# A two-layer relational graph convolution on one core: relation 0 treated like the other seven, and the root product moved to the end of each layer

## The reference

```
x: 1250 x 768, edges: 21250 (src, dst, type 0..7), sorted by dst
layer(x, W[8], root, b):
    sums[dst, r]  = sum of x[src] over the edges of type r that end in dst
    mean          = sums / max(count, 1)
    return sum_r mean[:, r] @ W[r]  +  x @ root + b
h   = relu(layer(x, W1, root1, b1))
out = layer(h, W2, root2, b2)
result = layernorm(x + out)
```

## Time and profile before

| | |
|---|---|
| median of 3 runs | 1470.09 us |
| the profiled execution, its own time | 1469.78 us |
| its span, first to last instruction | 1468.0 us |
| PE busy | 1451.5 us, 99% of the span |
| DVE busy | 983.4 us, 67% |
| ACT busy | 604.9 us, 41% |
| POOL busy | 572.6 us, 39% |
| HBM read and written | 204.47 MB and 65.49 MB |

### The profile page before, as it was taken

The page is one execution under the profiler, slowest core; times in us unless marked ns, Lnnn a source line. Parts: engine busy times, 40 slices in busy tenths (PEclk is TensorE's granted clock), DMA queues, the critical chain, the costliest instruction groups (busy, mean ns, idle before and its releaser), DMA issues.

```text
span 1468.0 us, 23940 instructions
## 1 busy us (share of the span) xinstructions
PE 1451.5 (99%) x8875; PEld 1438.4 (98%) x8875; DVE 983.4 (67%) x1604; ACT 604.9 (41%) x845; POOL 572.6 (39%) x457
## 2 busy tenths in 40 slices
PE   8999999999999999999999999999999999999998
PEld 8999999999999999999999999999999999999997
DVE  8899999857777677898740144545454454539887
ACT  4222344335444443566342233334343333417654
POOL 0000000066777774764306233434242424316553
PEclk9999999999999999999999999999999999999999
DMA  6453321358777786565337465646464656625454
GB/s 200 146 169 124 94 76 43 105 183 267 255 208 247 238 250 188 150 192 165 105 122 216 151 207 170 207 146 218 141 212 151 212 169 189 214 82 149 145 168 132
DMA packets 109595, 249.70 MB, mean 170 GB/s; under 512 B 20183, under 2 KB 83334, under 8 KB 109442
## 3 DMA queue, kind: packets, MB, share of 16 engines
q0 software_dynamic: 32480, 135.65, 31.5%
q1 hardware_dynamic: 77026, 112.88, 23.7%
HBM read 204.47 MB, written 65.49 MB: 184 GB/s over the span
## 4 chain that ended last, share of the span: by engine, by line
PE 94%; DMA 2%; DVE 2%; ACT 1%; issue 1%; SPq 0%; POOL 0%; ACTq 0%; POOLq 0%; DVEq 0%
PE prod L872 72%; PE agg L918 15%; PE agg L1039 2%; PE agg L872 2%; PE prod L863 1%; DMA raw<-y,bucket_index 1%; PE prod L918 1%; DMA y<-y_stage 1%; DVE g_low L1166 1%; PE agg L863 0%; DMA x_rows<-in_x 0%; PE agg L1042 0%; DVE g_low L1170 0%; ACT g_high L705 0%; DVE g_high L1166 0%
## 5 line engine op out<-in xcount | busy, mean ns | idle before, releaser
L872 PE MATMUL prod<-w_high,h_high 128*128 128x384 f32 x2100 | 707.8, 337 | 0.0
L872 PE MATMUL prod<-w_high,h_low 128*128 128x384 f32 x2100 | 702.5, 335 | 0.0
L872 PE MATMUL prod<-w_low,h_high 128*128 128x384 f32 x2100 | 701.8, 334 | 0.0
L590 POOL DMA_INDIRECT raw<-y,bucket_index x346 | 448.7, 1297 | 506.6 <-DVE g_low L1170 249.8
L1170 DVE TENSOR_TENSOR g_low<-raw,g_high 128x768 fp32r<-128x768 f32 x246 | 225.5, 954 | 300.7 <-ACT g_high L708 299.6
L741 ACT ACTIVATE y_stage<-prod 128x384 f32<-128x384 f32 x280 | 137.7, 492 | 679.5 <-PE prod L872 670.3
L872 PEld LDWEIGHTS prod<-w_high,h_high 128*128 128x128 f32 x2100 | 394.3, 188 | 0.3 <-issue 0.2
L872 PEld LDWEIGHTS prod<-w_low,h_high 128*128 128x128 f32 x2100 | 394.5, 188 | 0.0
L872 PEld LDWEIGHTS prod<-w_high,h_low 128*128 128x128 f32 x2100 | 394.2, 188 | 0.0
L708 ACT ACTIVATE g_high<-raw 128x768 fp32r<-128x768 f32 x266 | 211.6, 839 | 64.4 <-PE agg L918 46.2
L918 PE MATMUL agg<-g_high,one_hot 128*128 128x384 f32 x720 | 186.0, 339 | 4.2 <-DVE g_low L1170 2.7
(11 more groups left out here) (178 smaller groups left out, 1002.6 us busy)
## 6 DMA issues: line engine op xcount, KB each, us to landing
y<-y_stage SPq DMA_DIRECT2D x280, 168.0 KB
w_raw<-in_w_all SPq DMA_DIRECT2D x35, 1152.0 KB, 7.2
raw<-y,bucket_index POOLq DMA_INDIRECT x346, 4.8
y<-y_stage SPq DMA_DIRECT2D x280, 19.5 KB
y<-in_x SPq DMA_DIRECT2D x1, 3750.0 KB, 14.0
acc<-in_x POOLq DMA_DIRECT2D x10, 375.0 KB, 4.3
x_rows<-in_x SPq DMA_DIRECT2D x10, 336.0 KB
y<-acc SPq DMA_DIRECT2D x10, 336.0 KB
```

The lines of the kernel that those rows point to most:

```text
L590: pool.indirect_dma_start(raw_rows(slot), None, y[0:written * N, :], bass.IndirectOffsetOnAxis(ap=bucket_index[:, at_column:at_column + 1] ...
L872: mm = pe.matmul(to, left[:, k, t * P:(t + 1) * P], right[:, h, k, :], start=(k == 0 and left is h_high and right is w_high), stop=(n == 0 ...
```

## The change

All eight relations are multiplied first, stored, gathered and summed in the same way. Relation 0 has two blocks a tile like the others, and its overflow joins the two shared overflow blocks at the last relation. `average`, `keep`, the turns of the averages, the copy of x and the store of h are gone. Layer 1 is now q = 0 to 7 for relations 0 to 7 and q = 8 for the root; layer 2 is q = 9 to 16 and q = 17 for the root. Both root matrices have the form that only q = 17 had: halves interleaved tile by tile, and relation 7's sums added onto the same banks. The order of the first steps is another: three steps of half 0, two of half 1, and then the buckets of tiles 0 and 1 directly after one another. In layer 1 the finished tile goes through relu and is turned there, and POOL may load x over a tile of `acc` as soon as that tile is turned. In `finish`, DVE cuts the low parts of the next tile before the moments of the last.

The diff, cut to its core:

```diff
-    TILES = [FULL] * (R - 2) + [FULL + 1, FULL + OVER]
+    TILES = [FULL] * (R - 1) + [FULL + OVER]
-    ROOT1 = R - 1
-    MEAN1 = R
-    ROOT2 = 2 * R
-    MEAN2 = Q - 1
+    ROOT1 = R
+    ROOT2 = Q - 1
-        PAIRED = BEHIND[R - 2]
+        PAIRED = LAYER
...
         def last_part(s):
+            if s < 5:
+                return ((0, 0), (0, 1), (0, 2), (1, 0), (1, 1))[s]
+            if s == STEPS - 1:
+                return 1, T - 1
+            return 1 - s % 2, (s + 1) // 2 - (1 - s % 2)
         def last_pair(t):
+            return (agg[:, 0, :, 0:HALF], prod[:, 0:2, 0:HALF], prod[:, 2:4, 0:HALF])[t % 3]
         def finished(s):
+            h, t = last_part(s)
+            return [0, 1] if s == 4 else [t] if s > 4 and h == 1 else []
+        def finishing(layer):
             def actions(s):
+                todo = [("sum", layer * R + R - 1, R - 1, t) for t in finished(s)]
+                if layer == 0 and s > 4:
+                    todo += [("turn", 1, None, t) for t in ([0] if s == 5 else [n - 1 for n in finished(s)])]
                 return todo
...
-                if s == STEPS - 1:
-                    sp.dma_start(y[0:N, :], x).then_inc(x_copied, 16)
...
-            for t in range(T):
-                sp.wait_ge(relu_done, t + 1)
-                for rows in parts_of(t):
-                    sp.dma_start(y[t * NT + rows.start:t * NT + rows.stop, :], acc[rows, t, :]).then_inc(h_stored, 16)
...
-            gather_relation(R - 1, R - 1, stop=SOONER)
-            pool.wait_ge(x_copied, 16)
-            gather_relation(R - 2, 0, 1)
-            gather_spilled(0, R - 1)
-            gather_relation(R - 1, R - 1, start=SOONER)
+            gather_spilled(0, R - 1)
             wait_y(0, R - 1)
+            gather_relation(R - 1, R - 1)
             def load_residual(t):
+                pool.wait_ge(transposed, 2 * T + 2 * (t + 1))
                 pool.dma_start(acc[0:ROWS[t], t, :], x[t * NT:t * NT + ROWS[t], :]).then_inc(residual_loaded[t], 16)
-            pool.wait_ge(transposed, 6 * T)
-            pool.wait_ge(h_stored, 16 * PARTS * T)
...
+            def finish(layer):                     # ScalarE
+                q, g = (ROOT1, ROOT2)[layer], layer * R + R - 1
+                high_of_unit(q, 1)
+                high_spilled(layer, g)
+                bucket(g, 0)
+                for t in range(T):
+                    if layer == 0 and t == T - 2:
+                        high_of_unit(q + 1, 0, STEPS * q + FIRST_HALF)
+                    if t + 1 < T:
+                        bucket(g, t + 1)
+                    if layer == 0:
+                        relu(t)
+                        if t:
+                            high_of_turn(1, t - 1)
+                    else:
+                        deviation(t)
+                        if t + 1 < T:
+                            norm(t)
...
+            def finish(layer):                     # TensorE
+                for s in range(STEPS):
+                    last_step(layer, s)
+                    for what, a, _, t in finishing(layer)(s):
+                        if what == "turn":
+                            turn(a, t)
+                        else:
+                            bucket(a, t, last_pair(t))
+                    if s == 0:
+                        sum_spilled(layer, layer * R + R - 1)
...
-            def keep(k, t, h, bank):
-                dve.wait_ge(prod_done, k + 1)
-                a = acc[:, t, h * HALF:(h + 1) * HALF]
-                dve.tensor_tensor(a, prod[:, bank, 0:HALF], a, ALU.add).then_inc(root_kept, 1)
...
+            def finish(layer):                     # VectorE
+                q, g = (ROOT1, ROOT2)[layer], layer * R + R - 1
+                low_of_unit(unit(q, 1), 1)
+                add_spilled(layer, g)
+                prepare(g, R - 1, 0)
+                for t in range(T):
+                    if layer == 0 and t == T - 2:
+                        low_of_unit(unit(q + 1, 0), 0)
+                    if t + 1 < T:
+                        mark(g, R - 1, t + 1)
+                        cut_low(g, t + 1, 0, 1)
+                    add(g, R - 1, t)
+                    if t + 1 < T:
+                        cut_low(g, t + 1, 1)
+                    if layer:
+                        moments_of(t)
+                        if t + 1 < T:
+                            scale_of(t)
+                    elif t:
+                        low_of_turn(1, t - 1)
```

More of the change, by code:

```diff
@@ L843, in norm @@
                                scale=std[:, t % 2, 1:2]).then_inc(normed, 1)
-            last = 2 * R - 1
-            high_of_unit(MEAN2, 1)
-            high_of_turn(3, T - 1)
-            high_spilled(1, last)
-            bucket(last, 0)
-            for t in range(T):
-                if t + 1 < T:
-                    bucket(last, t + 1)
-                deviation(t)
-                if t + 1 < T:
-                    norm(t)
+            matrix(2, 2, after=copied_ahead(2))
+            matrix(3, 3, after=copied_ahead(3))
+            for q in range(TABLE_END, ROOT1 - 1):
+                matrix(q, q, pair_of(q))
+            matrix(ROOT1 - 1, ROOT1 - 1, one_relation(R - 2, None))
+            finish(0)
+            matrix(ROOT1 + 1, stored_before(1, 0), last_turns)
+            with act.Fori(1, R) as r:
+                matrix(r + ROOT1 + 1, stored_before(1, r), one_relation(r + R - 1, None))
+            finish(1)
         @block.tensor
@@ new lines, in sum_spilled @@
+                        with pe.Fori(0, NB) as key:
+                            pe.wait_ge(spill_low[layer], i + 1)
+                            pe.wait_ge(spill_hot[layer], i * NB + key + 1)
+                            for part in (g_high, g_low):
+                                for c in range(2):
+                                    mm = pe.matmul(agg[:, 1, c, 0:HALF], one_hot[:, 0, 0, :],
+                                                   part[:, 0, c * HALF:(c + 1) * HALF],
+                                                   start=part is g_high, stop=part is g_low, skip_group_check=True)
+                            mm.then_inc(spill_summed[layer], 1)
@@ L1064, in matrix @@
                         middle[1]()
-                    if bank is None:
-                        last_step(s)
-                    else:
-                        step(q, s, bank(s), free(s))
+                    step(q, s, free(s))
                     if after:
@@ L1196, in low_of_turn, with matrix @@
                     low_of_half(u, t, turned(n, hh, t))
-            def matrix(q, actions, keep_step=None, more=True, spilled=None, after=None,
-                       low_at=((2, 0, K), (12, 0, K))):
-                cut = SPILL_STEP[spilled[0]] if spilled else -1
-                order = [(s, a[1:]) for s in range(STEPS) for a in actions(s) if a[0] != "turn"]
+            def matrix(q, actions, low_at=((2, 0, K), (12, 0, K))):
+                order = [a[1:] for s in range(STEPS) for a in actions(s) if a[0] == "sum"]
                 ready = n = 0
-                def prepare_next():
-                    prepare(*order[n][1])
-                    return n + 1
                 for s in range(STEPS):
-                    if keep_step and not spilled and s == max(0, order[0][0] - EARLY):
-                        ready = prepare_next()
-                    if keep_step:
-                        keep_step(s)
                     for what, *a in actions(s):
@@ L1218, in matrix @@
                             continue
-                        ahead = n + 1 < len(order) and not (s <= cut < order[n + 1][0])
-                        for m in range(ready, n + 1 + ahead):
-                            prepare(*order[m][1])
-                        ready = n + 1 + ahead
+                        for m in range(ready, min(n + 2, len(order))):
+                            prepare(*order[m])
+                        ready = min(n + 2, len(order))
                         n += 1
-                        if what == "sum":
-                            if keep_step:
-                                dve.wait_ge(root_kept, (STEPS if q == MEAN1 else 0) + s + 1)
-                            add(*a)
+                        add(*a)
                     for at, first, stop in low_at:
```

433 lines of the change are left out of this document (110 added, 323 removed).

## The result

The kernel after takes 1461.05 us (median of 4 runs, 1460.23 to 1461.29). The kernel before, beside it on the same chip, takes 1470.05 us (4 runs, 1469.45 to 1471.24). The ratio is 0.9938 with a 95% interval of 0.9922 to 0.9954. So it is faster by 9.0 us, where I had forecast 19.1, and it lies 3 us above the upper end of my range.

What follows compares the result with a forecast made beforehand. PE, busy 1451.5 of 1468.0 us, was taken to bound the kernel; 1469.8 less 24.9 saved, plus 4.1 for tiles 0 and 1 and 2.0 for early x, gave 1451.0 us, range 1446 to 1458.

Steps and rivals of the forecast that it cites:

- The table: Edge-column table matmuls: 20 of 480 columns go in each of 170 groups, saving 1.4 us.
- -13.6: Turns of averages: twenty turns, ten in each layer, leave PE at 0.68 us each, saving 13.6 us.
- -6.9: Third blocks of relation 0: 40 summing matmuls leave PE, saving 6.9 us.
- -3.0: Dense sums in q = 7: waits for rows and low parts, and before a first turn, vanish, saving 3.0 us.
- Are relation 7's rows there in time?: Closing stages, tile 0: a gather chain of 15.5 us fits within 17.0 us, so it costs 0.
- Rival 4: Kernel becomes slower: relation 7's rows arrive late in both layers, up to 1474 us; chance 0.04.
- Tiles 0 and 1 directly after one another: +4.1: Closing stages: tile 1's parts are made only during tile 0's bucket, costing 2.0 us a layer, 4.1 with latencies.
- x loaded early in layer 1: +2.0: End of q = 8: POOL's bias adds fall on tiles 8 and 9 and may hold DVE, costing 2.0 us, bounds 0 to 6.4.
- The other tiles: 0: Closing stages' remaining tiles: cadence 8.68 us in q = 17, 9.36 in layer 1, hides DVE and ACT work; costs 0.
- the last tile ... may bring 0 to 1 us and is left out: Kernel's end: low parts cut before the moments may bring 0 to 1 us, left out of the sum.
- the second: Rival: POOL's adds hold tiles 8 and 9 fully, +6.4, or one layer's gathers are late; 1455 to 1458 us; chance 0.20.
- the third: Rival: layer 1's closing stage settles at a DVE or ACT cadence of 10.2 us; 1459 to 1463 us; chance 0.08.

Runs made afterwards that it cites:

- e7_spaced: Kernel after with x loaded late, q = 17 moments before three low parts except tile 0's, and tiles 0, 1, 2 summed one step apart in both closing stages: 1451.73 us.
- e8_layer1: Kernel after with x loaded late, q = 17 moments before three low parts except tile 0's, and tiles 0, 1, 2 spaced in q = 8 alone: 1451.17 us.
- e1_late: Kernel after, but POOL loads x only when all of h is turned, so its adds leave the closing stage: 1449.48 us.
- e4_moments: Kernel after, but in layer 2 alone DVE takes a tile's moments ahead of the next tile's last three low parts; x loads stay early: 1458.08 us.
- e9_norm: Kernel after with x loaded late and ACT taking the previous tile's norm just ahead of this tile's deviation; moments stay last: 1450.80 us.

## Why the prediction was wrong

**Right: what bounds it, and the savings.** PE did lose the work, and the span followed PE and its waits and nothing else. The table gave 1.5 us (I had 1.4): ten of its edge columns take 2.02 us in place of 2.11 from start to start, and there are 17 such bursts. The sums have 1400 matmuls at L810, 40 fewer. q = 7 takes 76.3 us, exactly what q = 10 to 16 take, so the dense sums' waits are gone with their arrangement. The steps after the turns of averages, "-13.6", "-6.9" and "-3.0", gave together 14.1 + 9.4 + 0.8 = 24.3 us where I had 23.5. The rest is 3.9 in q = 0 to 6, in place of 1.4; 1.7 of that is q = 6, whose first step had taken 4.30 us before and takes 3.12 after.

**Right: "Are relation 7's rows there in time?"** Bucket 0 starts without a wait in both layers. Rival 4 is out.

**Nearly right: "Tiles 0 and 1 directly after one another: +4.1".** 4.7 measured. The working was of the right kind, and e7_spaced and e8_layer1 take just this term away in q = 8 (2.35 us).

**Wrong: "x loaded early in layer 1: +2.0".** This is the step that failed. The mechanism was on the list, and the term was mis-sized: 10.8 us measured by e1_late, against my 2.0 and an upper bound of 6.4. The bound was wrong for two reasons. I had counted four instructions that can be held, the low parts of tile 9, since I thought of long instructions. In fact w_low was held (+1.5), two of the four selection matrices were held most of all (+6.0 for instructions of some 0.28 us), and of the four low parts only the two that stood beside an add (+2.3). An instruction on DVE that is held stands until POOL's add ends, however short it is itself, and one stood through two adds. So the bound has to be made from POOL's side: six adds, of 1.84 us when nothing holds them, fall on the stretch from 740 to 757 us, 11 us in all, and 9.8 us of holds were measured; for all ten adds it would have been 18.4. The second reason is the clock: the wait that this made was followed by matmuls at half the rate, 2.5 us more that no sum of waits contains. Together 9.8 of holds and 2.5 of clock, less the 1 us of cover in my working, are 11.3 by parts, beside 10.8 by stretches.

The case in rows 8 that I had taken as a weaker hold was a whole one: the DVE instruction on ten columns, with one input, stood until the memset ended. It already showed that a short instruction with one input waits out what is left of POOL's. The rule of the Trainium skill's page "SBUF — State Buffer" (Who interferes with whom) that I had set beside the trace pointed to the right side too, for the low parts.

**Wrong: "The other tiles: 0", for q = 17, and "the last tile ... may bring 0 to 1 us and is left out".** The cadence of 8.68 us before had the moments ahead of three low parts. I looked at how busy DVE and ACT are in a cadence, 6.7 and 5.2 us, and not at the order in which they wait for each other. With the moments last, the chain through both in turn is 8.79 us and longer than the cadence. That costs 0.8 us over seven tiles, and as the low parts come later than before, 1.2 at the last step and 2.1 in the tail. e4_moments and e9_norm both take it away, by opposite edits. For q = 8 the term was right: tiles 2 to 8 are 9.33 to 9.36 us apart, without a wait.

By my rivals the result is closest to the second ("the adds hold fully", 1455 to 1458), which had a chance of 0.20 and still too small a price. The measured 1461.05 lies within the figures of the third (1459 to 1463), but by luck: the cadence of q = 8 that it supposes, 10.2 us, isn't there. A cadence set by DVE and ACT came in q = 17 instead, and cost 0.8 us.

## What to carry to other kernels

When work is moved on an engine that can hold another, price it from the side of the engine that holds: each held instruction, a short one too, stands until the other engine's ends, so the price can come up to the whole time of the work that was moved. Gaps in that work are where the held ones get through. Where an order is changed on two engines that hand a tile back and forth, write down the closed loop and add its length; the busy share of each says nothing on it. And the cost of a wait of PE may not end with it: behind one of 4.8 us here, and behind ones of 2.0 us in e4_moments and e7_spaced, the granted clock was lower. Look at the windows behind each.

## What I had not expected of the hardware

- DVE and POOL: four selection matrices with one input in SBUF (128x128) went from 0.87 to 6.88 us beside POOL's adds; one of them took 4.69 us, over two adds, and two took their usual 0.28. POOL's short memsets held them too, each until it ended (1.77 us for four), but held no instruction with two inputs. DVE's add with one input in PSUM passed a POOL add unheld (0.94 us).
- The hold goes both ways: a POOL add that came while w_low ran took 3.64 us in place of 1.84.
- A wait of PE of about 5 us in a stage that is otherwise dense took the granted clock down: the windows from 750 us on had 0.67, 0.50 and 0.80, and PE's rate was back in full at 765. Waits of 2.0 us did it too (0.57 in e4_moments from 1380 us on; 0.84 and 0.73 in e7_spaced), while the two waits of a pair in q = 8, 0.48 and 0.76 us, did not.
- The table's third matmul at 60 columns in place of 80 was worth 1.5 us over 170 groups, 9 ns each, about the same per column as in the earlier trace rows: down to 60 columns the cost still follows the columns.
